# GpSimd issues the accumulating writes of an old block ahead of the gathers of a new one in four stages of a graph network

## The chip, the cores and the metric

One core of a Trainium2 chip runs the whole program. The metric is the device time of one execution in microseconds; the figure for the kernel is the median of its runs.

## What is computed

Four message-passing layers over a graph with 50,000 nodes of 160 features (64 scalars, 32 vectors of 3) and 25,000 edges, sorted by target, each followed by a residual and a layer norm. Layers 0 and 1 have this form, cut to what matters here:

```python
gs, gv = f_s[edge_src], f_v[edge_src]          # gather per edge
mid0 = w0 * gs * y0[:, None]                   # w: small MLP of the edge's attributes
mid1 = w3 * jnp.einsum('euc,ec->eu', gv, y1) * INV_SQRT3
mid2 = (w1 * gs)[:, :, None] * y1[:, None, :]
mid3 = w2[:, :, None] * gv * y0[:, None, None]
ns0, ... = segment_sum(mid0, edge_dst, N), ... # scatter-add per node
```

Layer 2 turns the messages into attention values (`a = exp(a - amax[edge_dst])`, divided by their sum, `segment_sum(vs * a, edge_dst)`), and layer 3 gathers at one end of each edge and sums at the other, as layers 0 and 1 do.

## The kernel before

All is fp32. A layer is an edge phase and a node phase; layer 2 has two attention phases in between. The stages run one after another with a barrier between them. Edges are cut into NB = 50 blocks of B = 512 (T = 4 rows for each of 128 partitions). Buffers of loaded and gathered data have R = 4 copies, most others 2.

Each stage is a software pipeline, written out by hand: `pipeline(eng, n, head, stages)` (line 130) gives an engine a list of pairs (lag, f), and in turn m the engine does f for block m - lag, in the order of the list. An engine runs its list in order, so a wait in one entry holds all behind it. Engines meet by counting semaphores alone.

In edge phases 0 and 1 (`edge_phase_01`, line 176) a block passes through these steps:

- SyncE `load` (lag 0): gather indices and attributes of block i, once the gathers of block i - 4 have landed and VectorE has used block i - 4. In phase 0 it also issues `clear_later` (L287): three DMAs in each turn that zero a fiftieth of the sum tables of the later layers.
- GpSimd `gather` (lag 0, L313): waits for the load and for rows of block i - 4 to be built, then issues 4 indirect DMAs, one for each of the T rows, that fetch 128 node rows each into `xg[i % 4]`.
- ACT `copy_scalars` (lag 1, L423), the first entry of ACT's turn, and VectorE `make_rows` (lag 1, L348 to L360), the last entry of VectorE's turn, wait for the 4 gathers of the block.
- TensorE turns the rows (L471), multiplies by weights (L490, L497) and forms messages (L506, L507); ACT copies (`weights` L444, `outputs` L451, `copies` L430, `hidden` L437); VectorE multiplies (L403) and builds the target comparison (L380).
- TensorE `sums` (lag 5, L519) adds up the edges of a block with one target; ACT `sums` (lag 5, L457) copies the result to `summed[i % 2]` once the writes of block i - 2 have landed.
- GpSimd `add` (lag 6, L330): waits for the cell indices, for the landing of the writes of block i - 1 (`added`) and for ACT's copy, then issues 4 accumulating indirect DMAs into the table `agg`.

Edge phase 3 (`edge_phase_23` with l = 3) has the same parts: `gather` (L918) waits for TensorE to have turned the rows of block i - 4 (L1177, L1180), which TensorE does as the last entry of turn i - 1; VectorE uses the gathered rows at lag 2; ACT's copy of the sums is L1159 at lag 6, `add` (L940) has lag 7. Edge phase 2 runs the same function but has no `add` and stays as it is.

The attention sum (`attention_sum_phase`, line 1646) gathers the maximum of each edge's target (L1708), VectorE subtracts it (L1730) and builds the comparison (L1736), ACT takes the exponent (L1753), VectorE weights the values (L1742), TensorE sums (L1771), ACT copies (L1758), GpSimd writes (L1718, lag 4).

What follows the last block of a stage is the drain: `add` alone, then a wait for all writes. The node phases read the table after that.

Of the kernel before, what the change touches and what calls it, by code (L numbers as in the profile page):

```python
# [114 lines left out]
def due(count):  # L115

    return max(count, 0) if isinstance(count, int) else count
# [23 lines left out]
def pipeline(eng, n, head, stages):  # L141

    tail = (n - 1) // R * R

    def at(m):
        for lag, f in stages:
            c = m - lag
            if 0 <= c < n:  # L150
                f(c, c % R, c // R, LASTP if c == NC else P)

    for m in range(head):
        at(m)
    with eng.Fori(head // R, tail // R) as j:
        for q in range(R):
            for lag, f in stages:
                f(R * j + (q - lag), (q - lag) % R, j + (q - lag) // R, P)
    for m in range(tail, n + max(lag for lag, f in stages)):
        at(m)  # L160
# [6 lines left out]
def edge_pipeline(eng, stages):  # L167
    pipeline(eng, NB, 3 * R, stages)
# [7 lines left out]
def edge_phase_01(nc, l, x, agg, dram, wt, later):  # L176
# [4 lines left out]
    with ExitStack() as ctx:  # L181
# [65 lines left out]
        def fence(eng):  # L247

            eng.sem_inc(turn, 1)
# [53 lines left out]
        @block.gpsimd  # L303
        def _(pool):
            def gather(i, r, k, parts):
                pool.wait_ge(loaded[r], 32 * (k + 1))
                fence(pool)
                pool.wait_ge(rows_v, due(4 * (i - 3)))
                fence(pool)
                pool.wait_ge(rows_a, due(i - 3))  # L310
                fence(pool)
                for t in range(T):
                    pool.indirect_dma_start(xg[r][:, t, :], None, x, bass.IndirectOffsetOnAxis(ap=gidx[r][:, t:t + 1], axis=0)).then_inc(gathered[r], 16)  # L313

            def add(i, r, k, parts):
                u = r % 2
                if l == 0:
                    pool.wait_ge(idx_ok, i + 1)
                    fence(pool)
                else:  # L320
                    pool.wait_ge(cidx_in[r], 16 * (k + 1))
                    fence(pool)
                pool.wait_ge(added, 16 * T * i)
                fence(pool)
                pool.wait_ge(sum_ok, i + 1)
                fence(pool)
                if l == 0 and isinstance(i, int) and i == 0:
                    pool.wait_ge(zeroed, 16 * (NA // P // ZR))
                for t in range(T):
                    pool.indirect_dma_start(agg, bass.IndirectOffsetOnAxis(ap=cidx[r][:, t:t + 1], axis=0), summed[u][:, t, :], None, compute_op=ALU.add).then_inc(added, 16)  # L330

            if l == 0:
                pool.memset(zero[:], 0.0).then_inc(zset, 1)
            edge_pipeline(pool, ((0, gather), (6, add)))
            pool.wait_ge(added, 16 * T * NB)

        @block.vector
# [434 lines left out]
def edge_phase_23(nc, l, x, agg, dram, wt):  # L772
# [10 lines left out]
    with ExitStack() as ctx:  # L783
# [81 lines left out]
        def fence(eng):  # L865

            eng.sem_inc(turn, 1)
# [41 lines left out]
        @block.gpsimd  # L909
        def _(pool):  # L910
            def gather(i, r, k, parts):
                pool.wait_ge(loaded[r], 16 * NS * (k + 1))
                fence(pool)
                pool.wait_ge(turned, due(2 * NS * (i - 3)))
                fence(pool)
                for s in range(NS):
                    for t in range(T):
                        pool.indirect_dma_start(xg[s][r][:, t, 0:XR], None, x, bass.IndirectOffsetOnAxis(ap=gidx[s][r][:, t:t + 1], axis=0)).then_inc(gathered[r], 16)  # L918

            def powers(s):  # L920

                def f(i, r, k, parts):
                    u = r % 2
                    pool.wait_ge(st_ok[s], 10 * (i + 1))
                    fence(pool)
                    pool.wait_ge(nrm[s], due(3 * (i - 1)))
                    fence(pool)
                    pool.tensor_tensor(rs[s][u][:], var[s][u][:], wt("mhalf8").rearrange("p (a t) -> p a t", a=2), ALU.pow).then_inc(rs_ok[s], 1)  # L928
                return f

            def add(i, r, k, parts):
                u = r % 2
                pool.wait_ge(idx_ok, i + 1)
                fence(pool)
                pool.wait_ge(added, 16 * T * i)
                fence(pool)
                pool.wait_ge(sum_ok, i + 1)
                fence(pool)
                for t in range(T):
                    pool.indirect_dma_start(agg, bass.IndirectOffsetOnAxis(ap=cidx[r][:, t:t + 1], axis=0), summed[u][:, t, :], None, compute_op=ALU.add).then_inc(added, 16)  # L940

            pool.wait_ge(y_ok, 3)
            pool.tensor_tensor(yn[:], yh[:], wt("mhalfn"), ALU.pow).then_inc(n_ok, 1)
            if l == 2:
                edge_pipeline(pool, ((0, gather), (1, powers(0)), (1, powers(1))))
            else:
                edge_pipeline(pool, ((0, gather), (7, add)))
                pool.wait_ge(added, 16 * T * NB)

        @block.vector  # L950
# [695 lines left out]
def attention_sum_phase(nc, dram, mx, agg, wt):  # L1646
# [3 lines left out]
    with ExitStack() as ctx:  # L1650
# [27 lines left out]
        def fence(eng):  # L1678

            eng.sem_inc(turn, 1)  # L1680
# [3 lines left out]
        @block.sync  # L1684
        def _(sp):
            def load(i, r, k, parts):
                sp.wait_ge(msg_ok, due(2 * (i - 3)))
                fence(sp)
                sp.dma_start(tidx[r][:], dram["dst_t"][bass.ds(i, 1)].rearrange("a p t -> (a p) t")).then_inc(loaded[r], 16)
                sp.dma_start(trow[r][:], dram["dst_r"][bass.ds(i, 1)].broadcast_to([P, B])).then_inc(loaded[r], 16)  # L1690
                sp.dma_start(val[r][:], dram["val"][bass.ds(i, 1)].rearrange("a p t c -> (a p) t c")).then_inc(loaded[r], 16)

            def load_late(i, r, k, parts):
                sp.wait_ge(added, due(16 * T * (i - 3)))
                fence(sp)
                sp.dma_start(cidx[r][:], dram["cidx"][bass.ds(i, 1)].rearrange("a p t -> (a p) t")).then_inc(late[r], 16)

            edge_pipeline(sp, ((0, load), (3, load_late)))

        @block.gpsimd  # L1700
        def _(pool):
            def gather(i, r, k, parts):
                pool.wait_ge(loaded[r], 48 * (k + 1))
                fence(pool)
                pool.wait_ge(dif_ok, due(i - 3))
                fence(pool)
                for t in range(T):
                    pool.indirect_dma_start(big[r][:, t, :], None, mx, bass.IndirectOffsetOnAxis(ap=tidx[r][:, t:t + 1].bitcast(U32), axis=0)).then_inc(big_in[r], 16)  # L1708

            def add(i, r, k, parts):  # L1710
                pool.wait_ge(late[r], 16 * (k + 1))
                fence(pool)
                pool.wait_ge(added, 16 * T * i)
                fence(pool)
                pool.wait_ge(sum_ok, i + 1)
                fence(pool)
                for t in range(T):
                    pool.indirect_dma_start(agg, bass.IndirectOffsetOnAxis(ap=cidx[r][:, t:t + 1], axis=0), summed[r % 2][:, t, :], None, compute_op=ALU.add).then_inc(added, 16)  # L1718

            edge_pipeline(pool, ((0, gather), (4, add)))  # L1720
            pool.wait_ge(added, 16 * T * NB)

        @block.vector
# [813 lines left out]
```

## Time and profile before

| | us |
|---|---|
| median of 3 runs | 8330.65 |
| lowest, highest | 8328.97, 8366.61 |
| the profiled execution | 8414.61 |
| its span | 8412.9 |

| busy, share of the span | us |
|---|---|
| TensorE | 6207.3 (74%) |
| VectorE | 5184.6 (62%) |
| GpSimd | 4877.7 (58%) |
| ACT | 2864.1 (34%) |

The profile is of one execution. Times are microseconds from the start of its span. PE is TensorE, PEld its weight loads, DVE VectorE, POOL GpSimd, SP or SPq SyncE and its DMA queue. L330 is line 330 of the kernel. A row of a timeline says when an instruction started, how long it took, and how long its engine had been idle before and what released it; the releaser is inferred. The time of a DMA_INDIRECT row is GpSimd's time to issue it; the data land later. The ends of matmuls are modelled and can come early. A row of the table by stage has the bounds and the length of a stage, then the busy time of PE, PEld, DVE, ACT and POOL in this order, each with its number of instructions. Stages: edge phase 0 from 92 to 862, edge phase 1 from 1429 to 2233, edge phase 2 from 2913 to 4068, attention sum from 5124 to 5790, edge phase 3 from 6837 to 7786.

### The profile page before, as it was taken

How to read it: one execution, taken by the hardware profiler on the slowest of the kernel's cores; microseconds unless marked ns; L12 is line 12 of the kernel's file. 1: busy time of each engine (PE TensorE's matmuls, PEld its weight loads, DVE VectorE, ACT ScalarE, POOL GpSimd, SP SyncE). 2: the span in 40 equal slices, each digit the busy share in tenths (PEclk: the TensorE clock that was granted, in tenths of full speed). 3: DMA queues.
4: the chain of work that ended last, by engine and by line, in shares of the span. 5: the costliest groups of instructions: out<-in, count | busy, mean ns of one | idle time of the engine just before them, and what ended most of it. 6: DMA issues, size and time to landing. Idle time of an engine off the chain costs nothing. (4 is left out here: it accounts for less than half of the span.)

```text
span 8412.9 us, 133573 instructions
## 1 busy us (share of the span) xinstructions
PE 6207.3 (74%) x31036; PEld 4735.4 (56%) x31036; DVE 5184.6 (62%) x16572; ACT 2864.1 (34%) x6687; POOL 4877.7 (58%) x5156
## 2 busy tenths in 40 slices
PE   4999565999776779999433333556999969999666
PEld 2666564666666534444333333555888846666565
DVE  2666575444487366666798992223888855555566
ACT  1333564333355433333100000002555533333455
POOL 3776565667544575555266666886666656665112
PEclk9999787999988887888655556777999979999888
DMA  7888554344466122222333323443222223333444
GB/s 268 214 212 220 156 179 144 60 63 63 97 206 190 58 59 52 51 54 52 129 123 125 124 94 82 74 74 63 100 97 98 97 60 65 64 64 51 160 168 161
DMA packets 600272, 940.65 MB, mean 112 GB/s; under 512 B 228072, under 2 KB 346472, under 8 KB 590328
## 3 DMA queue, kind: packets, MB, share of 16 engines
q1 hardware_dynamic: 417656, 783.53, 28.9%
q0 software_dynamic: 182400, 154.78, 13.3%
q8 instruction: 70, 1.15, 0.1%
q14 instruction: 146, 1.20, 0.0%
HBM read 569.65 MB, written 368.33 MB: 111 GB/s over the span
## 5 line engine op out<-in xcount | busy, mean ns | idle before, releaser
L330 POOL DMA_INDIRECT agg<-summed,cidx x400 | 658.0, 1645 | 362.4 <-ACT summed L457 229.9
L1640 PE MATMUL pm_m<-rep_m,same_m 128*128 128x9 f32 x1600 | 348.6, 362 | 651.3 <-DVE blk_m L1616 530.0
L918 POOL DMA_INDIRECT xg<-x,gidx x600 | 618.6, 1031 | 352.5 <-PE pt L1180 189.8
L1640 PEld LDWEIGHTS pm_m<-rep_m,same_m 128*128 128x128 f32 x1600 | 345.0, 332 | 655.1 <-issue 487.9
L1771 PE MATMUL pc_a<-msg_a,same_a 128*128 128x168 f32 x1600 | 347.5, 395 | 360.8 <-issue 247.7
L1056 DVE TENSOR_TENSOR pr<-pf,ws 128x512 f32<-128x512 f32 (+1 forms) x250 | 172.4, 689 | 654.3 <-PE pf L1195 442.9
L403 DVE TENSOR_TENSOR pr<-pf,ws 128x512 f32<-128x512 f32 x200 | 138.3, 692 | 673.0 <-PE pf L490 513.3
L1771 PEld LDWEIGHTS pc_a<-msg_a,same_a 128*128 128x128 f32 x1600 | 335.9, 262 | 372.3 <-issue 294.6
L519 PEld LDWEIGHTS pc<-ob,same 128*128 128x128 f32 x3200 | 441.5, 189 | 80.3 <-issue 80.3
L519 PE MATMUL pc<-ob,same 128*128 128x161 f32 x3200 | 465.4, 303 | 3.6 <-ACT summed L457 3.6
L940 POOL DMA_INDIRECT agg<-summed,cidx x200 | 363.3, 1816 | 104.2 <-issue 58.8
L612 PE MATMUL pta_n<-wsb,xr_n 128*128 128x128 f32 x784 | 147.8, 319 | 359.2 <-DMA ar_n<-agg 359.2
L623 PE MATMUL pk_n<-wsb,xta_n 128*128 128x160 f32 x1568 | 408.3, 346 | 1.5 <-DVE y_n L676 1.5
L1145 ACT ACTIVATE ob<-po 128x256 f32<-128x256 f32 (+1 forms) x400 | 148.7, 372 | 739.0 <-PE po L1220 592.2
L655 ACT ACTIVATE xn_n<-y_n,nr_n,rs_n 128x160 f32<-128x160 f32 x784 | 342.9, 511 | 149.0 <-POOL nr_n L767 148.8
L1195 PE MATMUL pf<-ts,wsb 64*128 64x512 f32 (+1 forms) x600 | 374.4, 740 | 18.0 <-issue 15.4
L928 POOL TENSOR_TENSOR rs<-var,wsb 128x8 f32<-128x8 f32 x100 | 183.0, 1831 | 338.8 <-DVE var L992 337.7
L1953 POOL TENSOR_TENSOR rs_n<-ve_n,wsb 128x4 f32<-128x4 f32 x98 | 98.7, 1007 | 483.3 <-DVE nm_n L1941 483.3
L1718 POOL DMA_INDIRECT agg<-summed_a,cidx_a x200 | 325.0, 1625 | 70.7 <-issue 59.7
L1582 DVE TENSOR_TENSOR masked_m<-arow_m,apart_m 128x1024 f32<-128x1024 f32 x150 | 365.6, 2491 | 0.0
L1753 ACT ACT_TABLE_LOAD x1 | 1.3, 1283 | 1061.5 <-PEq L126 1061.5
L1539 POOL DMA_INDIRECT mx<-new_m,cidx_m x200 | 195.0, 975 | 242.7 <-DVE new_m L1623 197.0
(295 smaller groups left out, 19476.1 us busy)
## 6 DMA issues: line engine op xcount, KB each, us to landing
arow_m<-att SPq DMA_DIRECT2D x50, 2048.0 KB
ar_n<-agg SPq DMA_DIRECT2D x194, 322.0 KB
x<-xn_n SPq DMA_DIRECT2D x194, 322.0 KB, 2.8
xr_n<-x SPq DMA_DIRECT2D x194, 322.0 KB
agg<-zero SPq DMA_DIRECT2D x50, 768.0 KB
ar_n<-agg SPq DMA_DIRECT2D x97, 384.0 KB
agg<-zero SPq DMA_DIRECT2D x50, 672.0 KB
ar_n<-agg SPq DMA_DIRECT2D x97, 336.0 KB
```

The costliest lines, as they stand in the source:

```text
L330: pool.indirect_dma_start(agg, bass.IndirectOffsetOnAxis(ap=cidx[r][:, t:t + 1], axis=0), summed[u][:, t, :], None, compute_op=ALU.add).th ...
L519: last = pe.matmul(pc[:, t, 0:W], same[u][:, s, t * P:(t + 1) * P], ob[u][:, s, 32:32 + W], start=(s == 0), stop=(s == T - 1))
L623: pe.matmul(pk[u][:, t, 0:D], xta[u][:, t * P:(t + 1) * P], wt(f"na_{l}"), start=True, stop=False)
L655: a.activation(xn[r][:, t, 0:D], y[u][:, t, :], ACT.Identity, bias=nr[u][:, t:t + 1], scale=rs[u][:, t:t + 1]).then_inc(xn_ok, 1)
L918: pool.indirect_dma_start(xg[s][r][:, t, 0:XR], None, x, bass.IndirectOffsetOnAxis(ap=gidx[s][r][:, t:t + 1], axis=0)).then_inc(gathered[r ...
L940: pool.indirect_dma_start(agg, bass.IndirectOffsetOnAxis(ap=cidx[r][:, t:t + 1], axis=0), summed[u][:, t, :], None, compute_op=ALU.add).th ...
L1195: last = pe.matmul(pf[:], wt(f"f{g + 1}_{l}{s}"), ts[r % 2][0:n, 2 * s + g, :], start=(s == 0), stop=(s == NS - 1))
L1539: pool.indirect_dma_start(mx[u], bass.IndirectOffsetOnAxis(ap=cidx[r][:, t:t + 1], axis=0), new[u][:, t, :], None).then_inc(sent[u], 16)
L1582: v.tensor_tensor(masked[:, t], arow[r][:, t * P * H:(t + 1) * P * H].rearrange("p (e h) -> p h e", h=H), apart[:, t, :].unsqueeze(1).to_b ...
L1640: last = pe.matmul(pm[:, T * t + s, :], same[u][:, s, t * P:(t + 1) * P], rep[u][:, s, :], start=True, stop=True)
L1718: pool.indirect_dma_start(agg, bass.IndirectOffsetOnAxis(ap=cidx[r][:, t:t + 1], axis=0), summed[r % 2][:, t, :], None, compute_op=ALU.add ...
L1771: last = pe.matmul(pc[:, t, 0:W], same[u][:, s, t * P:(t + 1) * P], msg[u][:, s, :], start=(s == 0), stop=(s == T - 1))
```

## The change

In each turn GpSimd now does `add` of its old block first and `gather` of its new block after it, in edge phases 0, 1 and 3 and in the attention sum. Lags, waits, buffers, the instructions and their number are the same.

```diff
--- before.py
+++ after.py
@@ -331,7 +331,7 @@
 
             if l == 0:
                 pool.memset(zero[:], 0.0).then_inc(zset, 1)
-            edge_pipeline(pool, ((0, gather), (6, add)))
+            edge_pipeline(pool, ((6, add), (0, gather)))
             pool.wait_ge(added, 16 * T * NB)
 
         @block.vector
@@ -944,7 +944,7 @@
             if l == 2:
                 edge_pipeline(pool, ((0, gather), (1, powers(0)), (1, powers(1))))
             else:
-                edge_pipeline(pool, ((0, gather), (7, add)))
+                edge_pipeline(pool, ((7, add), (0, gather)))
                 pool.wait_ge(added, 16 * T * NB)
 
         @block.vector
@@ -1717,7 +1717,7 @@
                 for t in range(T):
                     pool.indirect_dma_start(agg, bass.IndirectOffsetOnAxis(ap=cidx[r][:, t:t + 1], axis=0), summed[r % 2][:, t, :], None, compute_op=ALU.add).then_inc(added, 16)
 
-            edge_pipeline(pool, ((0, gather), (4, add)))
+            edge_pipeline(pool, ((4, add), (0, gather)))
             pool.wait_ge(added, 16 * T * NB)
 
         @block.vector
```

## Rows read from the trace of the kernel before

**Rows 1.** Table by stage: length, busy (instructions) by engine, clock, DMA share, GB/s.
```profile
92.00:862.00 770.00, 683.53 (x3300) 478.55 (x3300) 443.80 (x1450) 237.75 (x451) 536.84 (x400) 0.97 0.80 204
...
1429.00:2233.00 804.00, 727.73 (x3400) 476.52 (x3400) 332.16 (x900) 265.54 (x501) 529.86 (x400) 0.96 0.41 60
...
5124.00:5790.00 666.00, 347.47 (x1600) 335.88 (x1600) 148.96 (x400) 43.94 (x101) 528.15 (x400) 0.76 0.45 73
...
6837.00:7786.00 949.00, 840.83 (x3800) 591.29 (x3800) 522.10 (x1357) 334.80 (x950) 603.17 (x401) 0.94 0.36 60
```

**Rows 2.** Waits of GpSimd, attention sum: us in total, times, longest.
```profile
POOL agg L1718 <- ACT summed_a L1758: 8.3, 3, 2.8
```

**Rows 3.** Copies of the sums, edge phase 0: count, first and last start.
```profile
L457 ACT ACTIVATE summed<-pc x39: 707/707/708, 202.2 to 749.7; 128x644 f32<-128x644 f32 x39
```

**Rows 4.** Gathers and scalar copies, edge phase 0: count, last start.
```profile
L313 POOL DMA_INDIRECT xg<-in_x,gidx x100: 942/967/1437, 101.8 to 415.0; - x100
...
L423 ACT ACTIVATE rows<-xg x24: 411/420/432, 108.5 to 418.3; 128x256 f32<-128x256 f32 x24
```

**Rows 5.** Timeline of GpSimd, edge phase 0: start, duration, instruction, idle before, releaser.
```profile
403.15 1.62 POOL L330 DMA_INDIRECT agg<-summed,cidx  x1 [0.89 <-ACT summed L457]
...
415.00 0.95 POOL L313 DMA_INDIRECT xg<-in_x,gidx  x1 [0.30 <-issue]
```

**Rows 6.** Timeline of ACT, the same turn.
```profile
401.60 0.71 ACT L457 ACTIVATE summed<-pc 128x644 f32<-128x644 f32 x1 [5.39 <-PE pc L519]
...
403.60 0.41 ACT L423 ACTIVATE rows<-xg 128x256 f32<-128x256 f32 x1
403.91 0.59 ACT L444 ACTIVATE ws<-ph 128x512 f32<-128x512 f32 x1
...
416.78 0.71 ACT L457 ACTIVATE summed<-pc 128x644 f32<-128x644 f32 x1 [6.53 <-remote]
...
418.33 0.43 ACT L423 ACTIVATE rows<-xg 128x256 f32<-128x256 f32 x1
```

**Rows 7.** Timelines of GpSimd and ACT, first block of edge phase 0.
```profile
105.88 0.95 POOL L313 DMA_INDIRECT xg<-in_x,gidx  x1 [0.30 <-issue]
...
108.51 0.42 ACT L423 ACTIVATE rows<-xg 128x256 f32<-128x256 f32 x1 [89.99 <-DMA xg<-in_x,gidx]
```

**Rows 8.** Timeline of SyncE's DMA issues: zeroing of the later tables.
```profile
400.73 2.12 SPq L287 DMA_DIRECT2D agg<-zero  x3
...
785.78 1.79 SPq L287 DMA_DIRECT2D agg<-zero  x3
```

**Rows 9.** Timeline of GpSimd, last writes of edge phase 0.
```profile
795.90 1.81 POOL L330 DMA_INDIRECT agg<-summed,cidx  x1 [9.12 <-DMA agg<-summed,cidx]
...
808.09 1.55 POOL L330 DMA_INDIRECT agg<-summed,cidx  x1 [4.46 <-DMA agg<-summed,cidx]
```

**Rows 10.** Timeline of PE, the turn of rows 5 and 6.
```profile
405.24 1.12 PE L497 MATMUL ph<-hs,wsb 64*128 64x512 f32 x2
```

**Rows 11.** Timelines of GpSimd and ACT, a turn of edge phase 1.
```profile
1813.39 0.95 POOL L313 DMA_INDIRECT xg<-x,gidx  x1 [0.31 <-issue]
...
1817.30 0.42 ACT L423 ACTIVATE rows<-xg 128x256 f32<-128x256 f32 x1
```

**Rows 12.** Timelines of ACT and GpSimd, a turn of edge phase 3.
```profile
7219.74 0.81 ACT L1159 ACTIVATE summed<-pc 128x768 f32<-128x768 f32 x1 [4.78 <-DMA agg<-summed,cidx]
...
7226.78 1.99 POOL L940 DMA_INDIRECT agg<-summed,cidx  x1 [0.30 <-issue]
```

**Rows 13.** Timelines of VectorE and ACT, a turn of the attention sum.
```profile
5390.73 0.90 DVE L1742 TENSOR_TENSOR msg_a<-val_a,msg_a 128x256 f32<-128x256 f32 x2 [3.82 <-issue]
...
5398.20 1.69 DVE L1736 TENSOR_SCALAR same_a<-trow_a,tf_a 128x512 f32<-128x512 int32 x4 [0.81 <-PE pc_a L1771]
...
5402.72 0.73 ACT L1758 ACTIVATE summed_a<-pc_a 128x672 f32<-128x672 f32 x1 [12.02 <-DMA agg<-summed_a,cidx_a]
```

**Rows 14.** Waits of ACT in edge phase 3: us in total, times, longest.
```profile
ACT summed L1159 <- DMA agg<-summed,cidx: 134.2, 28, 4.9
```

## The prediction

> **What bounds the kernel now.** I read the table by stage first. The four stages that the change touches take 770 (edge phase 0), 804 (edge phase 1), 666 (attention sum) and 949 us (edge phase 3) [rows 1]. TensorE is busy 684 of 770, 728 of 804 and 841 of 949 us in the edge phases, and GpSimd 537, 530 and 603. In the attention sum TensorE has 347 of 666 and GpSimd leads with 528. Then the waits of GpSimd: in the attention sum its accumulating writes waited 8.3 us for ACT in all [rows 2]; what remains is issue, so GpSimd itself is the bound there. Last the pace of edge phase 0: 39 copies of the sums from 202.2 to 749.7 are 38 turns of 14.41 us [rows 3].
>
> **What the change does to the order.** Nothing is added or removed: 4 writes and 4 gathers are issued in each turn as before, and the instructions on GpSimd alternate, writes, gathers, writes, gathers, either way. What shifts is which block the gathers belong to. In edge phase 0 before, the gathers behind the writes of block j are those of block j+7; after, those of block j+6. The row counts 100 gathers, those of blocks 0 to 24, up to the one at 415.0, behind the writes of block 17 [rows 4, 5]. So **each gather is issued one turn later than now, in the same place between two groups of writes**. The question is who wants it, and when.
>
> **Edge phase 0.** In the turn shown ACT copies the sums at 401.60, the writes start at 403.15, and the last gather behind them is issued from 415.00 to 415.95 [rows 5, 6]: 14.35 us from copy to gather issued. These gathers are of block 24 now and will be of block 23. ACT's turn begins with the copy of the gathered scalars (L423), ahead of all else in its queue. That of block 23 is the 24th and starts at 418.33 [rows 4, 6], 2.38 us behind 415.95. So the slack, some 17 us today (2.38 and a turn), falls to 2.38 us, and the data must have landed in it.
>
> How long a landing takes isn't shown for a gather in this place. Without other traffic: the first block's last gather is issued from 105.88 for 0.95 us and ACT starts at 108.51, 1.7 us later [rows 7]. But here SyncE zeroes the later tables, three DMAs a turn, issued from 400.73 for 2.12 us [rows 8], and the DMA share is 0.80 against 0.41 in edge phase 1 [rows 1]. The nearest rows under that traffic are GpSimd's waits for its own writes at the phase's end: 9.12 us, when they ended at 786.78, 1 us behind a zeroing's first issue at 785.78, and 4.46 us for the next [rows 8, 9]. The zeroing is issued 0.9 us ahead of a copy of the sums (400.73, 401.60). If the turn stretches to some 15.6 us, it comes 14.7 us behind the previous copy, and the gathers, at 14.35, just ahead of it. Hence I take **5 us**, near the lower row, with 1.7 and 9.1 as ends.
>
> 5 us don't fit in 2.38, and a new loop closes over two turns: ACT's copy of the sums of block j, writes, gathers of block j+6, landing, ACT's copy of the scalars of block j+6, and from there through the turn to the copy of the sums of block j+2. From L423 to the next copy of the sums is a turn less the time from that copy to L423, 2.00 and 1.55 us in [rows 6], mean 1.8: 14.41 - 1.8 = 12.6. Of it 0.7 us gives, since the weights that ACT copies behind L423 end at 404.50 and TensorE, held by its own earlier work, goes on only at 405.24 [rows 6, 10]. Two turns are 14.35 + 5.0 + 12.6 - 0.7 = 31.25 us, a turn 15.6 instead of 14.41. The loop runs from block 6 to 49, some 43 turns: 43 x 1.2 = **+51 us**. With a landing of 1.7 us the floor is 13.98, below 14.41; but turns are uneven (15.2 in the rows, 14.41 in the mean) and a short one can stall: 0 to +13. With 6 us a turn is 16.1: +73; with 9.1 us 17.7: +140, which the stretched turn speaks against.
>
> The Trainium skill (DMA: Bandwidth & Descriptors, Anatomy of one DMA — SWDGE (gpsimd) path) gives a DMA from GpSimd a nearly constant cost of about 2.0 us, most of it completion. The quiet 1.7 us of [rows 7] agrees, the 9.12 us of [rows 9] does not. By that figure, an estimate, the floor of a turn would be 14.1 us and this phase would lose nothing: the first rival below. The same page (Queues, rings and completion order) lets a DMA engine go round its queues packet by packet, which speaks against a gather waiting for a whole zeroing.
>
> **Edge phase 1.** No zeroing runs here. The last gather behind a group of writes is issued by 1814.34, and the scalar copy that will need it starts at 1817.30 [rows 11]: 2.96 us for a landing of 1.7. **0 us**, with 1.3 us to spare; 0 to +15 if a landing takes 3 us.
>
> **Edge phase 3.** Here the gathers' condition (rows turned) comes at the same time as the writes' condition, and GpSimd waits for the gathers' first. Now: sums at 7219.74, then the gathers, then the writes at 7226.78, 7.04 us behind the sums [rows 12]. After: the writes about 1.6 us behind the sums (403.15 against 401.60 in edge phase 0), the gathers some 8 us later than now. That gains the writes 5.4 us, but the sums of a block wait only for writes two blocks back, a turn old; the gathers are used by VectorE two turns later. TensorE, at 841 of 949 us, stays the bound. **0 us**.
>
> **Attention sum.** GpSimd's work is the same and is the bound, so only the chain from gather to writes could hurt. The places of the gathers stay, the blocks are one older. VectorE's comparison, which follows a gather's landing, runs from 5398.20 to 5399.89; the weighting behind it (0.90 us) would then end by 5400.8. TensorE needs it when ACT has copied the previous sums, 5402.72 and 0.73 us [rows 13]. So 2.6 us remain: **0 us**. At the end the last gathers come between two groups of writes and cover a landing of some 2 us: **-2 us**. Edge phase 0's end likewise has 5 us of gathers inside the wait of 9.12 us, of which I credit 2: **-2 us**.
>
> **Sum.** 51 - 2 - 2 = +47 us on the profiled execution's 8414.61 (span 8412.9): 8462. That execution is 1.0% above the median of the runs, so for the median it is 8330.65 + 47 = **8378 us**, +0.57%.
>
> **Rivals.**
> 1. The landing beside the zeroing is short, or a slightly stretched turn moves the gathers ahead of it: in effect the new order is the old one. For: the quiet 1.7 us. Against: 9.12 and 4.46 us under the same traffic. Time: 8330.65 + (0 to 13) - 4 = 8327 to 8340. 30%.
> 2. Faster: the profile puts 134.2 us of ACT's waits in edge phase 3, 28 of them, down to the writes' DMA [rows 14]. If that were the cause, writes issued 5.4 us earlier would free 28 x 4.8 = 134 us: 8197. It decides where the landing of the writes, not TensorE's sums, comes last. Against: ACT waits for the writes of block i-2, a turn old; the name is only that of the last event. 6%.
> 3. Worse: the landing stays above 6 us and edge phase 1 loses its 1.3 us too: 73 to 140, + 15, - 4, about 8330.65 + 110 = 8440. For: the gathers then meet the zeroing every time. 9%.
> The forecast itself, +30 to +85 us, has 55%.
>
> **How the numbers follow.** A difference under 0.5% (42 us) can't be told from none here. Of the forecast's 55% a fifth lies under 42 us: slower 44 + 9 = 53%; within 11 + 30 = 41%; faster 6%. The range for 8 in 10 takes in rival 1 and the forecast, 8327 to 8425. The forecast's own range is 8361 to 8416.
>
> **What would show it.** Right: in edge phase 0 L423 waits for the gathers' DMA, some 2 us in most turns, and not in edge phase 1; turns of 15.6 us in edge phase 0; in edge phase 3 writes 1.6 us behind the sums with the stage still at 949 us; the attention sum at 664 us. Wrong: L423 without a wait (rival 1), edge phase 3 under 930 us (rival 2), edge phase 1 over 815 us (rival 3), or an attention sum in which GpSimd waits for ACT.

## Result and the profile after

The kernel after takes **8452.23 us** (median of 3 runs, 8442.23 to 8456.88) against 8330.65 us before: the ratio is 1.013, with an interval of 1.0086 to 1.0174. The forecast was 8378 us with a range up to 8425, so the sign was right and the loss was 122 us instead of 47. The profiled execution took 8442.23 us (span 8440.5). The profiled execution of before, at 8414.61, was 84 us above its own median. A part of that lies in edge phase 2, which the change doesn't touch: from its first gather to its last are 1015.0 us there and 982.3 us after. So the stages are compared one by one.

The table by stage of the kernel after, from the first gather of a stage to its last write (columns as in [rows 1]: bounds, length, busy us of PE, PEld, DVE, ACT, POOL, granted clock, DMA share, GB/s). The stages are edge phase 0, edge phase 1, the attention sum and edge phase 3:

```profile
102.00:969.00 867.00, 740.30 (x3300) 511.33 (x3300) 446.15 (x1450) 235.37 (x451) 532.25 (x400) 0.90 0.70 178
1537.00:2319.00 782.00, 728.40 (x3400) 477.48 (x3400) 331.09 (x900) 267.10 (x501) 529.55 (x400) 0.96 0.42 61
5176.00:5827.00 651.00, 344.82 (x1600) 333.24 (x1600) 140.54 (x400) 47.75 (x100) 519.14 (x400) 0.76 0.44 73
6912.00:7820.00 908.00, 840.85 (x3800) 591.40 (x3800) 525.05 (x1354) 334.64 (x950) 528.90 (x400) 0.96 0.39 62
```

The same view of the kernel before with the same kind of bounds. [rows 1] has wider bounds, by some 10 us in edge phase 0, 5 in edge phase 1, 6 in the attention sum and 38 in edge phase 3:

```profile
102.00:863.00 761.00, 683.53 (x3300) 478.55 (x3300) 443.80 (x1450) 237.75 (x451) 537.69 (x400) 0.96 0.79 203
1432.00:2231.00 799.00, 727.73 (x3400) 476.52 (x3400) 332.16 (x900) 265.54 (x501) 529.86 (x400) 0.96 0.41 60
5130.00:5790.00 660.00, 347.47 (x1600) 335.88 (x1600) 148.96 (x400) 42.66 (x100) 528.15 (x400) 0.76 0.45 72
6875.00:7786.00 911.00, 840.83 (x3800) 591.29 (x3800) 520.03 (x1354) 334.80 (x950) 570.12 (x400) 0.96 0.38 62
```

The loss is all in edge phase 0, 761 to 867 us. The attention sum gains 9 us and edge phase 3 is the same. Look at the granted clock of edge phase 0 too: it falls from 0.96 to 0.90, and TensorE's busy time rises by 57 us for the same 3300 matmuls. That is a cost which the forecast has no term for.

The pace, from the group of ACT's copies of the sums in edge phase 0 of the kernel after (count, first and last start), which answers to [rows 3]. 33 copies are 32 turns of 16.85 us, where it was 14.41:

```profile
L457 ACT ACTIVATE summed<-pc x33: 707/707/708, 207.0 to 746.2; 128x644 f32<-128x644 f32 x33
```

The time goes into waits, of ACT and of PE, here from 170 to 790 us in the kernel after (what waited for what: us in total, times, longest):

```profile
ACT rows L423 <- DMA xg<-in_x,gidx: 74.4, 19, 6.4
...
PE ph L497 <- ACT ws L444: 49.2, 17, 5.8
```

L423 waits for the gathers 19 times in 37 turns, so **in every second turn, for 3.9 us** of idle time, and TensorE waits for the copies of weights (L444) that are queued behind L423. In the kernel before, neither wait is there. Two turns of the kernel after show the alternation. First GpSimd's timeline (start, duration, instruction, idle before, releaser), with the last gathers of two turns:

```profile
403.80 0.95 POOL L313 DMA_INDIRECT xg<-in_x,gidx  x1 [0.31 <-issue]
...
418.36 1.18 POOL L313 DMA_INDIRECT xg<-in_x,gidx  x1 [0.30 <-issue]
```

Then ACT's timeline in the same turns:

```profile
405.26 0.71 ACT L457 ACTIVATE summed<-pc 128x644 f32<-128x644 f32 x1 [6.05 <-remote]
405.87 1.08 ACT L430 ACTIVATE ts<-pt 128x512 f32<-128x512 f32 x2
410.55 0.42 ACT L423 ACTIVATE rows<-xg 128x256 f32<-128x256 f32 x1 [3.61 <-DMA xg<-in_x,gidx]
410.88 0.58 ACT L444 ACTIVATE ws<-ph 128x512 f32<-128x512 f32 x1
...
422.27 0.71 ACT L457 ACTIVATE summed<-pc 128x644 f32<-128x644 f32 x1 [4.04 <-PE pc L519]
422.87 1.08 ACT L430 ACTIVATE ts<-pt 128x512 f32<-128x512 f32 x2
423.83 0.43 ACT L423 ACTIVATE rows<-xg 128x256 f32<-128x256 f32 x1
```

And the zeroing of the first of these turns, from SyncE's timeline of the kernel after; it answers to [rows 8]:

```profile
404.32 1.55 SPq L287 DMA_DIRECT2D agg<-zero  x3
```

The gathers issued by 404.75 have the zeroing right beside them, are there at 410.55, **5.8 us** later, and hold L423 up. The next ones, issued by 419.54, are ahead of their zeroing, and L423 at 423.83, 4.3 us later, has no wait. From 170 to 790 us the first kind ends 0.1 to 2.4 us behind the zeroing's first issue and takes 4.6 to 7.7 us to land, 5.8 in the mean; the second ends at least 1.4 us ahead of it and takes 1.6 to 2.1. (A landing is counted from the end of the last issue to the last update of the gathers' semaphore; ACT starts up to 0.1 us later.)

### The profile page after: what moved, and what is told of

It reads as the page before. It is cut to its first block and busy times, and to the rows that moved or that the text cites. A ratio compares the mean times of both kernels' runs of the same rounds, so it can differ in the third digit from the quotient of the medians.

```text
span 8440.5 us, 133573 instructions
## 1 busy us (share of the span) xinstructions
PE 6225.9 (74%) x31036; PEld 4746.5 (56%) x31036; DVE 5188.8 (61%) x16572; ACT 2865.4 (34%) x6687; POOL 4822.7 (57%) x5156
## 3 DMA queue, kind: packets, MB, share of 16 engines
q1 hardware_dynamic: 417656, 783.53, 28.9%
## 5 line engine op out<-in xcount | busy, mean ns | idle before, releaser
L330 POOL DMA_INDIRECT agg<-summed,cidx x400 | 651.5, 1629 | 465.6 <-ACT summed L457 356.5
L519 PEld LDWEIGHTS pc<-ob,same 128*128 128x128 f32 x3200 | 453.2, 194 | 83.6 <-issue 83.6
L940 POOL DMA_INDIRECT agg<-summed,cidx x200 | 326.4, 1632 | 300.1 <-ACT summed L1159 248.7
L519 PE MATMUL pc<-ob,same 128*128 128x161 f32 x3200 | 477.1, 308 | 1.9 <-ACT summed L457 1.9
```

Source lines behind the costliest of these rows:

```text
L519: last = pe.matmul(pc[:, t, 0:W], same[u][:, s, t * P:(t + 1) * P], ob[u][:, s, 32:32 + W], start=(s == 0), stop=(s == T - 1))
```

## The experiments

Each group of kernels ran beside runs of the kernel before on the same chip, and chips differ: its median was 8330.65 us above, and 8162.51, 8136.85 and 8399.57 us in the three groups below. In the first two groups edge phase 0 takes 699 us, not 761, so their turns are 13.07 us (copy of the sums to L423 1.56 us, L423 to the next copy 11.51) instead of 14.4. (The kernel before was profiled in the second of them; in the first, the same order of edge phase 0 stands in experiment 1.) Ratios are to the kernel before of the same group. Stage times go from first gather to last write and are of one profiled execution each, so a sum of stage differences can be some 30 us from a difference of medians.

**1. Only the edit of edge phase 0 undone.** From the kernel after:

```diff
-            edge_pipeline(pool, ((6, add), (0, gather)))
+            edge_pipeline(pool, ((0, gather), (6, add)) if l == 0 else ((6, add), (0, gather)))
```

> The new order in edge phases 1, 3 and the attention sum, the old one in edge phase 0. Theory A (the loss is all in edge phase 0, where the gathers land beside the zeroing): 8330 us less some 2 to 8 for the end of the attention sum, so 8320 to 8335, and edge phase 0 at 850 us as before. Rival B (the loss is spread, since the profile of before was itself a long execution): half of the loss stays, about 8390.

Measured: 8128.43 us, ratio 0.9976 (0.9939 to 1.0013). Edge phase 0 takes 699 us, edge phase 1 758, edge phase 3 905 and the attention sum 646. Without the edit of edge phase 0 nothing of the loss is left, and the point estimate is a small gain. (The 850 us that were expected for edge phase 0 "as before" are a slip: it was 761 us.)

**2. Only the edit of edge phase 0 done.** From the kernel before:

```diff
-            edge_pipeline(pool, ((0, gather), (6, add)))
+            edge_pipeline(pool, ((6, add), (0, gather)) if l == 0 else ((0, gather), (6, add)))
```

> The new order in edge phase 0 alone. Theory A: the whole loss of 110 to 125 us, 8440 to 8455, with L423 waiting for the gathers in every second turn. Rival B: 60 us, 8390.

Measured: 8301.78 us, ratio 1.0167 (1.0104 to 1.023); edge phase 0 takes 867 us. The whole loss comes from this one edit. The medians differ by 139 us and the stage by 867 - 699 = 168 us, more than the 106 us of the first pair, because the undisturbed turn is shorter on this chip while the stalled stage isn't. ACT's waits from 170 to 790 us:

```profile
ACT rows L423 <- DMA xg<-in_x,gidx: 112.3, 19, 6.7
```

Again 19 waits, of 5.9 us each. This trace also shows what a stall does to TensorE. Below is the table of busy times in stretches of 4 us around one of them, of the kernel with only this edit (columns as above); L423 waits in it from 404.8 to 410.6:

```profile
400.00:404.00 4.00, 4.00 (x31) 3.83 (x31) 2.50 (x6) 0.90 (x2) 3.08 (x4) 1.00 0.53 120
404.00:408.00 4.00, 3.19 (x12) 1.71 (x11) 0.00 (x0) 0.79 (x2) 3.39 (x3) 1.00 0.99 305
408.00:412.00 4.00, 0.37 (x1) 0.29 (x2) 0.48 (x1) 1.29 (x3) 3.39 (x3) 0.99 1.07 330
412.00:416.00 4.00, 4.00 (x7) 1.65 (x6) 3.93 (x16) 0.60 (x1) 3.08 (x4) 0.50 0.55 68
416.00:420.00 4.00, 4.00 (x10) 2.06 (x9) 3.60 (x13) 0.81 (x2) 1.63 (x2) 0.50 0.23 49
420.00:424.00 4.00, 4.00 (x16) 4.00 (x16) 0.84 (x2) 0.28 (x1) 0.00 (x0) 0.50 0.67 198
424.00:428.00 4.00, 4.00 (x26) 3.83 (x25) 0.00 (x0) 0.76 (x2) 0.00 (x0) 0.80 0.99 349
428.00:432.00 4.00, 4.00 (x15) 2.15 (x14) 1.73 (x5) 2.21 (x5) 2.90 (x2) 1.00 0.36 77
```

TensorE is nearly idle from 407 to 412 us. Then it works at 0.50, its 1.2 GHz, for three whole stretches and part of a fourth, and is back at 2.4 GHz at 428. So this stall of 6 us is followed by some 14 us of work at half the clock. It is one of the two longest stretches: over the 19 stalls from 170 to 790 us, 7.0 us at 1.2 GHz follow each in the mean. For the sum, from copy to copy: a pair of turns is 7.57 us (copy of the sums to stalled L423) + 13.30 (to the next copy) + 1.6 + 11.5 = 33.98 us against 2 x 13.07 = 26.14. The 7.8 us are 6.0 of stall less 1.4 that the chain can give, and 3.2 of slower clock that reach the chain. (The 1.4 and the 3.2 are read from the leg between L423 and the next copy of the sums: 11.51 us without a stall, 10.07 behind a stall at the full clock, as experiments 3 and 4 have it, and 13.30 here.) 21.5 pairs x 7.8 = 168 us, which is the difference of the stages, 867 - 699.

**3. The zeroing held back behind the gathers.** From the kernel after; SyncE issues a turn's zeroing only when the gathers of that turn have landed:

```diff
+                sp.wait_ge(gathered[r], upto(16 * T * (k + 2), 16 * T * ((NB - 1 - r) // R + 1)))
+                fence(sp)
                 for n in (1, 2, 3):
```

> The new order in all four stages, and the zeroing of edge phase 0 also waits until the gathers of the block whose gathers are in flight have landed. Theory A: a gather now lands in 1.7 us in each turn, two turns are 14.4 + 1.7 + 0.1 + 12.5 = 28.7 us, under the 28.9 of two turns before, so the loss is gone but for up to 15 us of uneven turns: 8325 to 8350. Rival C (the shift by a turn costs it, whatever the landing): 8452 as with the zeroing where it was, or more, since the zeroing now ends later.

Measured: 8219.74 us, ratio 1.0065 (1.0035 to 1.0095); edge phase 0 takes 746 us, clock 0.97. ACT's waits from 170 to 790 us:

```profile
ACT rows L425 <- DMA xg<-in_x,gidx: 90.1, 39, 7.5
```

Of the 168 us that the order costs, 121 are gone, though the order is the new one: most of the cost is the meeting with the zeroing. But 47 us remain. L423 (L425 here) now waits in nearly every turn, 39 times in 44, 2.3 us each, because a landing still takes 3.0 us on average (1.7 to 3.9). The loop is then 14.4 + 3.0 + 0.1 + 10.1 = 27.6 us for two turns, above this chip's 26.14; over 43 turns that is 31 of the 47 us. The stage's last L425 waits 7.5 us, which is 8 more. The expectation had reckoned with the first chip's turn, 28.9 for two, and was wrong there.

**4 and 5. Stalls of ACT without any gather moved.** From the kernel before: in every second turn of edge phase 0 ACT first makes two copies that nothing uses, 3.66 us in all, ahead of L423 (two tiles and a semaphore are declared for them).

```diff
             def copy_scalars(i, r, k, parts):
+                if l == 0 and r % 2 == 0:
+                    a.wait_ge(filled, 2 * (2 * k + r // 2))
+                    for n in range(2):
+                        a.activation(filler[n][:], wt("before"), ACT.Copy).then_inc(filled, 1)
```

> The old order, and in edge phase 0 ACT does two copies of 128 x 2048, some 3.7 us together, ahead of L423 in every second turn: the delay that the gathers cause, without moving a gather. Theory D (a delay of ACT there costs its length and, on top, time at the lower TensorE clock behind the stall): 25 x (3.7 - 0.7) = 75 us and 25 to 40 us more of a lower clock, so 8430 to 8445, and half as much again or more of time at the lower clock in edge phase 0. Rival E (it costs its length alone): 75 us, 8405. Rival F (the turn absorbs it): under 8360.

Measured: 8233.38 us, ratio 1.0092 (1.0054 to 1.013); edge phase 0 takes 771 us, +72, clock 0.96. Each of 22 turns is longer by the stall, and the trace holds both kinds of them: in 9 the clock stays up and the turn is 2.2 us longer (3.66 - 1.4), in 12 it is 3.8 us longer and in one 7.1. So 22 x 2.2 = 48 us are the stalls alone, and the clock adds 24. The sum, 72 us, is the 75 that rival E had for the length alone, and that is chance: theory D's 3.7 - 0.7 us for a stall was too much. What decides between them is the clock. Here are three legs, from L423 (L429 here) to the next copy of the sums, in the view of the table by stage; as many matmuls run in each, 49. TensorE's idle time ahead of them is the same too, 2.1 us; the clock falls behind 12 of 21 such holes between 170 and 790 us:

```profile
350.35:360.44 10.09, 9.03 (x49) 6.83 (x50) 8.76 (x29) 2.99 (x8) 7.13 (x6) 1.00 0.72 182
378.66:390.39 11.73, 10.67 (x49) 8.01 (x50) 8.79 (x29) 2.98 (x7) 7.69 (x7) 0.85 0.66 173
466.91:481.93 15.02, 13.96 (x49) 10.81 (x50) 8.76 (x29) 2.98 (x8) 7.13 (x6) 0.66 0.78 210
```

Was the clock's part in experiment 2 then an effect of the stall's length, or of something else in the new order? For that the kernel before ran once more with a profile in the next group, and the stall was doubled with four copies in place of two, 7.36 us.

> The kernel before, unchanged, for a profile on the chip of this group. Expected: edge phase 0 at a constant turn of 13.1 us where the TensorE clock is at its upper level and 15 us or so where it falls, the attention sum at 671 to 673 us and edge phase 1 at 767 to 809.

> The old order, with four copies of 128 x 2048 ahead of L423 in every second turn of edge phase 0, so that ACT stands still there about as long as it waits for the gathers in the new order (7.4 against some 6 us). No gather is moved. Theory D (time at the lower TensorE clock comes from the stall, whatever stalls): edge phase 0 costs 25 x (7.4 - 1.4) = 150 us and a further 40 to 70 us from the clock, with about 180 us of the stage at the lower level, so 8162 + 190 to 220. Rival G (the lower clock comes with the new order itself, its gathers and writes): time at the lower level stays near the 85 us of the two copies, and the cost at 150 to 165 us.

Measured: the kernel before took 8168.54 us in one run. With four copies it is 8343.18 us, ratio 1.0253 (1.0214 to 1.0293). The table by stage for edge phase 0, first of the kernel before in this group:

```profile
102.00:801.00 699.00, 663.77 (x3300) 467.01 (x3300) 442.19 (x1450) 234.71 (x451) 529.81 (x400) 0.99 0.84 221
```

Of the kernel with only the edit of edge phase 0:

```profile
102.00:969.00 867.00, 734.22 (x3300) 504.36 (x3300) 443.70 (x1450) 234.83 (x451) 532.18 (x400) 0.90 0.69 178
```

Of the kernel with four copies:

```profile
102.00:988.00 886.00, 714.21 (x3300) 486.53 (x3300) 443.69 (x1450) 407.30 (x547) 531.68 (x400) 0.90 0.66 174
```

A stall of 7.36 us in every second turn, with the old order and no late gather, costs 187 us and pulls the clock to 0.90, just as the new order does: 173 us of the stage are at 1.2 GHz, where rival G wanted 85. (Of the slower clock 2.1 us a stall reach the chain here, against 3.2 in experiment 2: here nearly 7 us at 1.2 GHz follow each stall, there 3 to 14.) The timeline of ACT in that kernel shows one of the stalls; L432 is its copy of the scalars, L466 its copy of the sums:

```profile
418.73 0.71 ACT L466 ACTIVATE summed<-pc 128x644 f32<-128x644 f32 x1 [4.04 <-PE pc L528]
...
420.29 3.72 ACT L426 ACTIVATE filler<-wsb 128x2048 f32<-128x2048 f32 x2
424.04 3.71 ACT L429 ACTIVATE filler<-wsb 128x2048 f32<-128x2048 f32 x2
427.65 0.40 ACT L432 ACTIVATE rows<-xg 128x256 f32<-128x256 f32 x1
```

So the lower clock follows from the periodic stall, whatever makes it. That the gathers or their order lower the clock in another way isn't needed.

**6 and 7. The zeroing taken into edge phase 1.** Edge phase 1 has the same two orders and no zeroing. Here the tables 2 and 3 are zeroed there as well (work that the reference doesn't need), in the first kernel with all orders as before, in the second with the new order everywhere but in edge phase 0. Cut to what matters; a tile of zeros is set up there too:

```diff
-                for n in (1, 2, 3):
+                for n in ((1, 2, 3) if l == 0 else (2, 3)):
...
-                edge_pipeline(sp, ((0, load), (3, load_late), (5, load_cidx)))
+                sp.wait_ge(zset, 1)
+                edge_pipeline(sp, ((0, load), (3, load_late), (5, load_cidx), (7, clear_later)))
+                sp.wait_ge(cleared, 32 * NB)
```

> The old order; SyncE zeroes two of the later tables a second time, in edge phase 1, 1440 KB in each turn, as edge phase 0 does with three. Theory A (the traffic matters only where a gather is awaited at once): the gathers have some 16 us, so edge phase 1 stays at 767 to 810 us and the total within 15 us of before. Rival H (the traffic itself slows the stage): 20 us or more.

> The same second zeroing, with the new order in edge phases 1, 3 and the attention sum and the old one in edge phase 0. Theory A: edge phase 1, which lost nothing under the new order without the traffic (769 against 767 us), now shows the pattern of edge phase 0. Two turns are 14.35 + 5 + 0.1 + 12.1 = 31.5 us against 28.4 of two turns at 14.2, so 43 x 1.6 = 67 us, with the lower clock 70 to 110 us, L423 waiting in every second turn; less 10 us in the attention sum. Rival C (the shift alone decides, and edge phase 1 is safe from it): within 15 us of the run with the old order.

Measured: the old order with zeroing takes 8163.57 us, ratio 1.0024 (0.9981 to 1.0068), the new one 8189.76 us, ratio 1.0058 (1.0014 to 1.0102). Edge phase 1 takes 759 and 790 us; without zeroing it was 756 to 758 us under the old order and 758 under the new one. ACT's waits in edge phase 1 of the second kernel:

```profile
ACT rows L426 <- DMA xg<-x,gidx: 76.1, 38, 4.4
```

Zeroing alone costs nothing and the order alone costs nothing; together they cost 31 us. It takes both, as the mechanism says. The size fell short of the expectation: a landing takes 4.6 us here, the chain gives 1.6 us (the leg from L426 to the next copy of the sums is 11.66 us without a stall and 10.07 behind one), the waits are 2.0 us each, and the clock stays at 0.96.

**8 and 9. L423 moved out of the way.** In ACT's turn of edge phases 0 and 1 the copy of the scalars goes from the first place to the one in front of the copy of the sums, behind the copies of weights, outputs and hidden rows, with the new order of GpSimd in one kernel and the old one in the other:

```diff
-            edge_pipeline(a, ((1, copy_scalars), (3, weights(0)), (4, outputs(0)), (3, weights(1)), (4, outputs(1)), (2, hidden(0)), (5, sums))
+            edge_pipeline(a, ((3, weights(0)), (4, outputs(0)), (3, weights(1)), (4, outputs(1)), (2, hidden(0)), (1, copy_scalars), (5, sums))
```

> The new order in all four stages; in edge phases 0 and 1 ACT copies the gathered scalars (L423) behind its hidden-layer copy, in front of the copy of the sums, and no longer first in its turn. Theory A, second part (a late gather costs so much because its first reader stands at the head of ACT's queue, ahead of work that TensorE waits for): that place lies some 7.5 us later, in 4 us that ACT spends idle, so a landing of 6 us fits; VectorE's rows, the other reader, have about 6.4 us and just fit. Edge phase 0 back at 700 to 715 us from its first gather to its last write, against 867 with the new order and 699 with the old; time at the lower clock at 40 to 60 us; total 8140 plus 0 to 15, less 12 in the attention sum. Rival I (the stall moves to VectorE's rows or to TensorE's turning of them): 780 us or more in that stage.

> The same move of L423 under the old order. Theory A: no gather is late there and L423 is 0.4 us in front of the copy of the weights, of which TensorE's slack of 1.4 us takes all: edge phase 0 stays at 699 us, total within 0.4% of before. If L423's 0.4 us were on the path, 43 x 0.3 = 13 us less in each of edge phases 0 and 1.

Measured: with the new order 8369.51 us, ratio 0.9972 (0.9957 to 0.9988); with the old one 8412.9 us, ratio 1.0018 (1.0003 to 1.0034). The table by stage, edge phase 0, first with the new order and late copy:

```profile
102.00:846.00 744.00, 674.76 (x3300) 473.52 (x3300) 444.44 (x1450) 239.17 (x451) 538.46 (x400) 0.98 0.83 207
```

Then with the old order and late copy:

```profile
102.00:863.00 761.00, 681.10 (x3300) 477.40 (x3300) 443.06 (x1450) 238.72 (x451) 533.66 (x400) 0.97 0.80 203
```

ACT's timeline in the new order and late copy, one turn; its last gather was issued from 404.89 to 405.84:

```profile
406.72 0.71 ACT L457 ACTIVATE summed<-pc 128x644 f32<-128x644 f32 x1 [5.88 <-remote]
407.33 1.08 ACT L430 ACTIVATE ts<-pt 128x512 f32<-128x512 f32 x2
408.28 0.62 ACT L444 ACTIVATE ws<-ph 128x512 f32<-128x512 f32 x1
...
416.41 0.59 ACT L437 ACTIVATE hs<-ph 64x512 f32<-64x512 f32 x1 [0.59 <-issue]
416.90 0.41 ACT L423 ACTIVATE rows<-xg 128x256 f32<-128x256 f32 x1
```

L444 goes on at once, and L423 has 11 us for the landing, which takes 5.8 us in the mean. From 170 to 790 us L423 waits 4 times, 7.1 us in all, of which 5.6 are one wait, and the new order turns from 1.3% slower, on the first chip, to 0.3% faster than the kernel before. The kernel after itself wasn't run on this chip. So the lateness of the gathers costs next to nothing by itself; it cost because their first reader stood at the head of a queue that TensorE lives on.

Edge phase 0 is 17 us shorter here than under the old order. The traces show where: on this chip and on the first one, ACT's copy of the sums often starts 1 to 3 us behind the modelled end of TensorE's sums (L519), for example in [rows 6] at 416.78 against 414.19, with "remote" as releaser. In all other profiles it starts 0.10 us behind that end. From 200 to 745 us these delays add up to 30 us with the new order and late copy, and to 49 us with the old one. Why TensorE's sums end late on two chips, and later under one order, isn't shown.

## Why the prediction was right in its sign and wrong in its size

**Each gather one turn later, right in front of its reader: right.** Experiments 1 and 2 put the whole loss on this edit in edge phase 0, 6 and 7 show that it takes both the order and the zeroing, and 8 shows that the reader's place decides.

**The landing beside the zeroing: right, a little small.** I took 5.0 us; the stalled turns show 5.8 in the mean in the kernel after and 6.2 in experiment 2, and the ends of 1.7 and 9.1 held. The trace of before had the figure, in the updates of the gathers' semaphore: its landings in edge phase 0 take 5.4 us in the mean, and nothing waits for them. The Trainium skill (DMA: Bandwidth & Descriptors, Anatomy of one DMA — SWDGE (gpsimd) path) gives some 2.0 us of fixed cost. This case agrees where nothing else runs, 1.7 us, and for the gathers that end ahead of the zeroing, and disagrees by 3.8 us beside it. Rival 1, whose time followed from such a landing, falls.

**The failed step: 12.6 - 0.7 us from L423 to the copy of the sums.** This term took TensorE's pace behind a stall as it was without one, and so put the clock at nothing. The trace of after has 13.2 us in the mean for this leg in the 19 stalled turns, instead of 11.9, since TensorE works at 1.2 GHz behind each stall. The leg goes with the length of that stretch, as in the rows of experiment 4: 11.2 to 11.8 us in the eight turns with some 3 us at 1.2 GHz, 11.7 to 13.4 in the six with some 7, 16.7 us in the four with 14. Behind a stall at the full clock it is 10.1 us on the other chips. So the term hid two errors of opposite sign, and it is luck that they nearly cancel: it was 1.8 us too long for a leg at the full clock (the chain gives 1.4 us, not 0.7, and the mean turn of 14.41 holds the late ends of TensorE's sums told in experiment 8), and it lacked 3.1 us of clock. With the landing, the two turns of after are 14.4 + 5.9 + 13.2 = 33.5 us, predicted 31.25; the 33 copies above give 33.7. For 21.5 pairs the miss is 2.45 x 21.5 = 53 us, of which the leg is some 28 and the landing some 19, and 51 + 53 = 104 us is the loss of the stage, 867 - 761, but for 2 us. The rows on which it could have been seen were there: the clock of 0.96 and 0.76 in [rows 1] beside TensorE's idle times. No rival named the clock either, and rival 3 came to 8440 by other terms: it wanted a landing above 6 us in every turn and a loss in edge phase 1, and the landing was 5.8 us in the mean and edge phase 1 lost nothing.

**"Some 2 us in most turns": wrong in form.** The loop runs over two turns, and only one of the two has to wait; the other keeps its gathers ahead of the zeroing. It is 3.9 us in every second turn. The mean pace could still be computed from the pair, but few long stalls take more of the clock along than many short ones: from 170 to 790 us TensorE is at 1.2 GHz for 133 us in experiment 2, with 19 waits of 5.9 us, and for 24 us in experiment 3, with 39 of 2.3 us.

**Edge phase 1: right.** 756 to 758 us under either order in the first two groups. The 17 us that it gains in the first pair of profiles are matched by the late ends of TensorE's sums told in experiment 8, 53 us in all before and 34 after; in the first two groups, where the sums don't end late, the order changes nothing.

**Edge phase 3: right.** GpSimd's timeline of the kernel after, which answers to [rows 12]; the sums of this block were copied at 7236.18, so the writes come 1.66 us behind, not 7.04:

```profile
7232.28 0.99 POOL L918 DMA_INDIRECT xg<-x,gidx  x1 [0.30 <-issue]
7237.84 1.63 POOL L940 DMA_INDIRECT agg<-summed,cidx  x1 [4.57 <-ACT summed L1159]
```

The stage stays at 905 to 918 us under both orders in all groups; in the wider bounds of [rows 1] it is 946 us after and 949 before. Rival 2 falls. ACT's waits of the kernel after, from 7000 to 7700 us, answer to [rows 14]:

```profile
ACT summed L1159 <- PE pc L1231: 198.4, 40, 6.5
```

Before, these waits were split, 134.2 us put down to the writes' DMA and 59.3 us to TensorE, 193.5 in all. With the writes out of the way they are as long and all TensorE's: the name in [rows 14] was only that of the last event.

**Attention sum: the sign right, too small.** -2 us was forecast. The stage takes 645.8 to 651.3 us in the five kernels with the new order and 657.1 to 660.6 in the seven with the old one: -9 to -13 us within a group. In the table by stage GpSimd's own busy time falls by 9.0 us (528.15 to 519.14) for the same 400 issues. The kernel after's group of the gathers, count and duration (least, median, most):

```profile
L1708 POOL DMA_INDIRECT big_a<-mx,tidx_a x200: 940/947/1987, 5175.7 to 5788.8; - x100
```

The kernel before's:

```profile
L1708 POOL DMA_INDIRECT big_a<-mx,tidx_a x200: 940/981/1989, 5130.5 to 5742.3; - x100
```

The median falls by 34 ns and the mean by 41 (1018 to 977 ns), which is 8 us over 200 gathers. Since GpSimd is the bound there, this reaches the time. I had held its work to be the same; why an issue gets shorter behind the writes isn't shown.

**The end of edge phase 0, -2 us:** it can't be read apart from the 106 us and wasn't tried by itself.

## What to carry to other kernels

When a transfer is issued later, find its first reader and ask what is queued behind that reader: here some 6 us of landing cost 106 to 168 us in a stage with the reader at the head of ACT's queue, and nothing that shows with it behind the copies that TensorE waits for. Where the rhythm of a full TensorE gets a periodic hole of some microseconds, add a term for the clock behind it; in experiment 2 it was 3.2 of the 7.8 us that each pair of turns lost. When a loop closes over two turns, compute the pair and expect one long stall in it, not two short ones.

## What the runs showed of the hardware

- **Periodic stalls lower TensorE's clock.** On the chips of the first two groups the granted clock of edge phase 0 is 0.99 without stalls, 0.96 with 3.66 us and 0.90 with 6 or 7.36 us in every second turn. The same leg of the loop takes 10.1 us at the full clock and 11.7 to 16.7 us with 3 to 14 us at 1.2 GHz in it.
- **A gather's landing depends on what is issued beside it.** The same 4 gathers land in 1.7 us when they end 1.4 us or more ahead of the zeroing, in 4.6 to 7.7 us when they end 0.1 to 2.4 us behind its first issue, and in 3.0 us when the zeroing waits for them.
- **The same kernel has another pace on another chip.** Edge phase 0 of the kernel before takes 699 us at a clock of 0.99 on one and 761 us at 0.96 on another, and the stalled order takes 867 us on both: the loss is larger on the chip where the kernel before is faster. Of the 62 us, 42 are the delays of ACT's copy of the sums, up to 3.0 us behind the modelled end of TensorE's sums, on the slower chip (200 to 745 us), and the faster one has none; some 18 are the clock (55 us of the stage at 1.2 GHz against 18).
